# A four-layer network on one core: two sums of the scan moved to GpSimd, its linear terms reordered, the expert result read out in four pieces, and two fp32 matrix stages of the retrieval layer made of half-precision products

## The chip, the cores and the metric

The kernel is one program for one core of one Trainium2 chip. The engines are TensorE (PE in the profile, its weight loads PEld), VectorE (DVE), ScalarE (ACT), GpSimd (POOL) and SyncE (SP, which here only issues transfers). The metric is device time in microseconds from the first to the last instruction, as the median of a few runs.

## The reference, cut to what matters

The whole is a residual network of four layers over a token tensor of 8 x 256 x 512 (`XT` in the kernel, channels on partitions). The change touches layers 1 and 2.

```
x = x + L0_ffn(L0_cond(x, ...))                 # attention and a mixture of experts, untouched
x = x + L1_ffn(L1_cond(cond, x))                # GRU over 256 steps, then a base matrix plus one of 8 low-rank experts
x = x + L2_ffn(L2_cond(cond, cond, x))          # FitzHugh-Nagumo network over 256 steps, then retrieval
x = x + L3_ffn(L3_cond(x, ...))                 # untouched

# L2_cond: for each of 256 steps, classical Runge-Kutta with four evaluations of
#   dq = q - q**3/3 - p + drive + tanh(q) @ coupling.T + bias ;  dp = EPS*(q + ALPHA - BETA*p)
# q and p are clipped to +-20; the sequence of q goes on.
# L2_ffn (8 heads, 4096 = 64 x 64 experts):
h  = silu(q_seq @ W_up.T + b_up)                # 512 -> 2048, "wide layer"
h  = h @ W_down.T + b_down                      # 2048 -> 256
sim -> top 8 of 64 twice -> top 8 of 64 pairs -> indices, softmax(sc)
z   = silu((h . down_embed[indices]) * softmax)
out = sum of z * up_embed[indices]              # 64 picked rows of 512 per token
```

## The kernel before, in words

**The scan (function `scan`, lines 576 to 970).** The GRU of layer 1 and the network of layer 2 run in one loop of 256 steps. The GRU and layer 1's experts are 17 steps ahead (`LEAD`): 17 GRU steps run alone, then each of 256 common steps `t` does step `t` of the network and GRU step `s=t+17`. State is 32 numbers on each of 128 partitions (4 blocks of channels x 8 sequences). All matrices are products of fp16 halves: with `hi` and `lo` parts, 16 matmuls of 32 columns with the low weights ("low") and 16 with the high weights ("high").

One evaluation `k` (0 to 3) is a ring: ScalarE takes two tanh of the new `q` (`kx` in fp16 L748, `Tt` in fp32 L749) and the square (L753); TensorE multiplies `kx` by the low weights (L639); VectorE forms the low half of tanh (`low_part`, L889); TensorE multiplies both halves by the high weights (L642); meanwhile VectorE computes the cubic term (`cubic`, L892), adds the linear terms and writes the sum beside the products in PSUM (`total`, "k_ps" rows of L807); then VectorE adds the three parts (`end`, TENSOR_REDUCE, L900) and the next evaluation starts. In the gaps TensorE runs the 96 matmuls of the three GRU gates in batches of 24, 28, 28 and 16 behind evaluations 0 to 3, then a share of layer 1's experts. The linear terms (`K2`, `X`, `W`, `Q`, `B0`, `G0`) are sums of `q` and `p` of the step, prepared one by one on VectorE between the others. All this is in program order on each engine, so the order of the VectorE statements in the loop (lines 906 to 968) decides when `total` and `end` run. The GRU's new state (`state_half`, L845) opens the batch behind evaluation 0.

Layer 1's experts work on blocks of 8 steps (`TL=8`; i = s mod 8): router and low-rank matmuls at i = 0 and 1, base matrix at i = 0 to 4, on VectorE the choice of the expert at i = 2 and 3 (`experts`, L855 to L864, both parts ahead of `end` of evaluation 2), a transpose at i = 3, the expert matrix at i = 5 and 6, and at i = 7 ScalarE copies the result of 256 columns from PSUM (`expert_out`, L738, behind evaluation 1), whereupon GpSimd adds it into `XT` (`results`, L778).

GpSimd's queue in a step: `E0` (needs the new `p`), two operations for the next drive (`D`, `Ds`), and one copy of `q` into the sequence buffer `HQ` (L799).

**Retrieval (function `retrieve_experts`, lines 972 to 1326).** After the scan, three parts, all of whose TensorE work is in fp32. (1) 8 slices of 256 tokens: `up` (512 matmul records of 256 columns a half, L1048), `down` (L1061), `similar` (L1069), while VectorE picks the best keys. (2) 16 tiles of 128 tokens: dense products with `down_embed` (`dense`), picking by one-hot matmuls (`pick`). (3) 16 tiles: for tile i+1, `scatter` spreads the 64 weights of each token over 4096 rows (one-hot matmuls, L1107, four quarters a tile) and ScalarE copies the result to SBUF (`spread`, two operations a quarter, L1175); for tile i, `combine` multiplies that by the whole `up_embed` table (L1117, 32 chunks of rows x 4 blocks of channels). TensorE's order is scatter(i+1,q), combine(i,q) for q = 0 to 3. VectorE writes the one-hot tables (`pairs_hot`, L1288, four a tile) and, once all four scatters of tile i+1 are done, the weight table `AW` for the next tile (`weights_hot`, L1293 and L1294), on which the next scatter waits. The table `ue` (8 loads of 1 MB) arrives while the last picks run.

## Time and profile before

| | us |
|---|---|
| median of 3 runs | 4984.41 (4960.73 to 4988.18) |
| the profiled execution | 4976.67 |
| its span, first to last instruction | 4975.1 |
| TensorE busy | 4722.6 (95%) |
| VectorE busy | 2745.3 (55%) |
| ScalarE busy | 1688.9 (34%) |
| GpSimd busy | 435.9 (9%) |

TensorE is busy nearly everywhere, but matmuls are pipelined and a busy TensorE need not be the one that sets the time: in the scan the four engines pass the state round in a ring. The span has these stages: up to 1012 us layer 0, the gates' input products and the GRU's lead; 1012 to 2821 us the common scan (in its last 17 steps there are no gates); 2821 to 3227 us part (1) of the retrieval, to 3605 part (2), to 4231 part (3) with the part's start up to 3679; then layer 3.

### The profile page before, as it was taken

Reading aid. Unit: us, or ns where it says so; the run is one execution under the profiler, and the core shown is the slowest. Engines: PE = TensorE matmul, PEld = TensorE weight load, DVE = VectorE, ACT = ScalarE, POOL = GpSimd, SP = SyncE. Lnnn points to the kernel's source line nnn. Section 1 sums busy time; section 2 is a strip of 40 time slices with the busy share of each in tenths; the row PEclk is TensorE's granted clock in tenths of the full one; section 3 lists DMA queues with packets and bytes.
Section 4 is the critical chain, followed back from the end, with each engine's and each line's share of the span. In section 5 each row is a group of like instructions: output and inputs, shape, how many; then the busy total and the mean of one; then the engine's idle time right before and its main releaser. Section 6 shows DMA issues by size and latency. Waiting matters only on the chain. (4 is left out here: it accounts for less than half of the span.)

```text
span 4975.1 us, 200432 instructions
## 1 busy us (share of the span) xinstructions
PE 4722.6 (95%) x85104; PEld 3682.8 (74%) x85104; DVE 2745.3 (55%) x15135; ACT 1688.9 (34%) x7079; POOL 435.9 (9%) x1163
## 2 busy tenths in 40 slices
PE   8999989599999999999999799999999999999999
PEld 3435654489989999999998687789999999344444
DVE  4110011488888889888888545665543431344421
ACT  1101111145555555555555322233322221243320
POOL 1000010311111111111111100000000000000000
PEclk8899989799999999999998699999989999899999
DMA  3202430000000000000001000033310000100000
GB/s 102 98 25 87 169 123 22 15 5 5 5 5 5 5 5 5 5 5 5 5 5 55 13 10 1 36 90 92 98 58 3 3 3 2 47 9 8 10 7 34
DMA packets 52304, 159.81 MB, mean 32 GB/s; under 512 B 13873, under 2 KB 14001, under 8 KB 46272
## 3 DMA queue, kind: packets, MB, share of 16 engines
q1 hardware_dynamic: 45408, 130.70, 8.0%
q8 instruction: 662, 10.85, 0.9%
q0 software_dynamic: 3712, 12.29, 0.8%
q10 hardware_dynamic: 2304, 4.20, 0.2%
q14 instruction: 218, 1.79, 0.1%
HBM read 129.63 MB, written 17.17 MB: 30 GB/s over the span
## 5 line engine op out<-in xcount | busy, mean ns | idle before, releaser
L639 PE MATMUL k_ps<-k_hx,k_wlo 128*128 128x32 f16 x16384 | 585.2, 178 | 90.8 <-ACT k_hx L748 78.0
L639 PEld LDWEIGHTS k_ps<-k_hx,k_wlo 128*128 128x128 f16 x16384 | 490.2, 97 | 158.6 <-ACT k_hx L748 97.6
L642 PE MATMUL k_ps<-k_hl,k_whi 128*128 128x32 f16 x16384 | 578.0, 177 | 6.1 <-issue 3.9
L642 PEld LDWEIGHTS k_ps<-k_hl,k_whi 128*128 128x128 f16 x16384 | 496.0, 96 | 11.7 <-issue 8.6
L639 PE MATMUL g_ps<-g_HX,g_wlo 128*128 128x32 f16 x12240 | 426.0, 177 | 35.5 <-DVE g_HX L845 33.3
L642 PE MATMUL g_ps<-g_HL,g_whi 128*128 128x32 f16 x12240 | 425.3, 177 | 14.4 <-DVE g_HL L813 12.5
L639 PEld LDWEIGHTS g_ps<-g_HX,g_wlo 128*128 128x128 f16 x12240 | 361.3, 96 | 51.1 <-DVE g_HX L845 35.9
L642 PEld LDWEIGHTS g_ps<-g_HL,g_whi 128*128 128x128 f16 x12240 | 363.2, 96 | 17.1 <-DVE g_HL L813 12.7
L748 ACT ACTIVATE k_hx<-k_q 128x32 f16<-128x32 f32 x768 | 176.1, 229 | 529.3 <-DVE k_q L900 529.3
L1517 DVE TENSOR_REDUCE t_NM<-t_ps 128x1 f32<-128x512 f32 x256 | 165.0, 686 | 218.3 <-PE t_ps L1383 218.3
L1288 DVE TENSOR_TENSOR HQ<-p_ior,p_pm 128x2048 f32<-128x2048 f32 x61 | 139.4, 2290 | 218.5 <-PE p_sim L1107 218.5
L490 DVE TENSOR_TENSOR m_hT<-GRZ,m_ps 128x256 f32<-128x256 f32 (+1 forms) x72 | 36.6, 508 | 386.0 <-ACT GRZ L453 386.0
L1117 PE MATMUL p_dn<-wm,GRZ 128*128 128x128 f32 x2048 | 241.7, 280 | 2.0 <-ACT wm L1175 2.0
L1117 PEld LDWEIGHTS p_dn<-wm,GRZ 128*128 128x128 f32 x2048 | 235.6, 195 | 3.4 <-ACT wm L1175 2.2
L1117 PE MATMUL p_pq<-r_mem,GRZ 128*128 128x128 f32 x2048 | 236.3, 276 | 0.0
L751 ACT ACTIVATE k_hl<-k_hx 128x32 f16<-128x32 f16 x1024 | 234.1, 229 | 0.0
L1117 PEld LDWEIGHTS p_pq<-r_mem,GRZ 128*128 128x128 f32 x2048 | 230.9, 192 | 1.1
L900 DVE TENSOR_REDUCE k_q<-k_ps 128x32 f32<-128x96 f32 x768 | 197.2, 257 | 54.8 <-PE k_ps L642 34.2
L1048 PE MATMUL p_up<-HQ,GRZ 128*128 128x256 f32 x1024 | 225.2, 382 | 1.8 <-PEq L22 1.8
L753 ACT ACTIVATE k_sq<-k_q 128x32 f32<-128x32 f32 x1024 | 221.8, 217 | 2.0 <-DVE k_q L905 1.1
L1048 PEld LDWEIGHTS p_up<-HQ,GRZ 128*128 128x128 f32 x1024 | 196.4, 192 | 29.1 <-issue 1.9
L889 DVE CUSTOM_DVE_ANT_0 k_hl<-k_T,k_hx 128x32 f16<-128x32 f32 x1024 | 194.3, 190 | 28.4 <-ACT k_T L749 3.6
(359 smaller groups left out, 9252.9 us busy)
## 6 DMA issues: line engine op xcount, KB each, us to landing
GRZ<-expert_places SPq DMA_DIRECT2D x64, 512.0 KB, 5.0
wm<-in_w_dram SPq DMA_DIRECT2D x4, 2816.0 KB, 9.9
...
```

The source lines that it names most:

```text
L490: V.tensor_tensor(hT[0:M,m,0:n],sA[0:M,st,0:n],ps[st*2+1][0:M,0:n],ALU.mult).then_inc(s_h,1)
L639: T.matmul(P(j),lo[:,kc,(m0+j)*128:(m0+j+1)*128],bc(x[:,kc,:].unsqueeze(1),[128,4,NB]),start=(j==0 and kc==0),stop=False,skip_group_check= ...
L642: i=T.matmul(P(j),hi[:,kc,(m0+j)*128:(m0+j+1)*128],bc(x(kc).unsqueeze(1),[128,2,2,NB]),start=False,stop=kc==KC-1,skip_group_check=True)
L748: A.activation(kx[:],m4(src),ACT.Tanh,scale=uq[k]).then_inc(k_hi,1)
L751: A.activation(kl[:,:,0,:],kx[:],ACT.Copy,scale=S).then_inc(k_hS,1)
L753: A.activation(sq[:],q[:,k,:],ACT.Square,scale=uq[k]).then_inc(k_sq,1)
L889: V.tensor_tensor_reduce(kl[:,:,1,:],m4(Tt[:]),kx[:],S,0.0,ALU.subtract,ALU.max,lz[:,0:1]).then_inc(k_lo,1)
L900: V.tensor_reduce(qn[:] if k==3 else q[:,k+1,:],ksum(k),AX.X,ALU.add).then_inc(k_q,1)
L1048: x=T.matmul(psu[n%2][:,(m%2)*256:(m%2+1)*256],wup[:,dd,m*128:(m+1)*128],HQ[:,dd,s*256:(s+1)*256],start=dd==0,stop=dd==3)
L1117: x=T.matmul(pso[i%2][:,dd*128:(dd+1)*128],ue[:,cc,dd*128:(dd+1)*128],Ws[i%2][:,cc,:],start=cc==0 and dd==0,stop=cc==31,skip_group_check=True)
L1288: V.tensor_tensor(B0[q] if i==0 else Bp[:,q],bc(ior[:].unsqueeze(1),[128,16,128]),bc(PM[:,i,1,q*16:(q+1)*16].unsqueeze(2),[128,16,128]),AL ...
L1517: V.tensor_reduce(NM[:,qc,hh*64+32:hh*64+33],psX[hh][:,:],AX.X,ALU.max,negate=True).then_inc(s_mx,1)
```

## The change

Scan:

```diff
 # GpSimd
-    G.tensor_copy(HQ[:,:,:,t-1],m4(q[:,0,:])).then_inc(k_out,1)
+    state_out(t-1)
+ e.wait_ge(k_b,t*2+1)
+ G.tensor_tensor(K2[:],Q[:,0,:],B0[:,0,:],ALU.add).then_inc(k_kx,1)
+ e.wait_ge(k_b,t*2+2)
+ G.tensor_tensor(X[:,0,:],Q[:,0,:],B0[:,1,:],ALU.add).then_inc(k_kx,1)
  results(t+LEAD)
+def state_out(t):
+    if t>0: e.wait_ge(k_ol,t)
+    G.tensor_scalar(qs[:],q[:,0,:],uq[0]*SQ,None,ALU.mult).then_inc(k_out,1)
+    e.wait_ge(k_out,t+1)
+    G.tensor_copy(HP[:,:,:,t,0],m4(qs[:])).then_inc(k_oh,1)
+    e.wait_ge(k_oh,t+1)
+    G.tensor_tensor(HP[:,:,:,t,1],m4(qs[:]),HP[:,:,:,t,0],ALU.subtract).then_inc(k_ol,1)
 # VectorE, evaluation 0
-    pre(s-1,Z_); limit(t-1); arg(s-1,Z_); low_part(t,0); diff(s-1)
-    G0; Q0; upd(s-1); cubic(t,0); state_half(s-1); total(t,0)
+    pre(s-1,Z_); limit(t-1); low_part(t,0); arg(s-1,Z_); diff(s-1)
+    G0; Q0; cubic(t,0); upd(s-1); total(t,0); state_half(s-1)
     end(t,0)
 # evaluation 1
-    ...; low(s); K2; X0; cubic(t,1); Q2; total(t,1); W0; end(t,1)
+    ...; low(s); cubic(t,1); e.wait_ge(k_kx,t*2+1); Q2; total(t,1); end(t,1)
 # evaluation 2
-    X1; W1; low_part(t,2); pre(s,R_); arg(s,R_); cubic(t,2); X2; total(t,2); W2; experts(s,0); experts(s,1); end(t,2)
+    W0; e.wait_ge(k_kx,t*2+2); X1; low_part(t,2); W1; pre(s,R_); cubic(t,2); arg(s,R_); X2; total(t,2); experts(s,0); end(t,2)
 # evaluation 3
-    pn; X3; hid_n(s); low_part(t,3); reset(s); cubic(t,3); cand(s); p; total(t,3); end(t,3)
+    W2; X3; hid_n(s); low_part(t,3); reset(s); pn; cubic(t,3); cand(s); total(t,3); p; experts(s,1); end(t,3)
 # TensorE: the transpose of the experts
-    if i==3: base(7,11); e.wait_ge(l_ht,j+1); T.transpose(...)
-    if i==4: base(11,16)
+    if i==3: base(7,11)
+    if i==4: base(11,16); e.wait_ge(l_ht,j+1); T.transpose(...)
 # ScalarE: masked(s) at i==5 (was 4); expert_out(s,k) behind the square of every evaluation k, 64 columns each
-    A.activation(ex[:]...,pso[:,0:KC*TN],ACT.Copy,scale=US).then_inc(l_e,1)
+    A.activation(ex[:,dc]...,pso[:,dc*TN:(dc+1)*TN],ACT.Copy,scale=US).then_inc(l_e,1)
 # GpSimd: results(s) waits for the fourth piece, e.wait_ge(l_e,4*j+4)
```

`HP` is the buffer `HQ` seen as pairs of fp16 numbers, high and low, so neighbouring tokens of one half are 4 bytes apart.

Retrieval:

```diff
 # before part (1): W_up is split in place, chunk by chunk (4 chunks of 2048 elements a partition)
+for x in range(4):                       # ScalarE; waits for the VectorE step of chunk x-1
+    A.activation(wpair(x)[:,:,0,:],wup[:,:,x*512:(x+1)*512],ACT.Copy,scale=SW).then_inc(s_wh,1)
+for x in range(4):                       # VectorE
+    V.scalar_tensor_tensor(wpair(x)[:,:,1,:],wup[:,:,x*512:(x+1)*512],SW,wpair(x)[:,:,0,:],ALU.mult,ALU.subtract).then_inc(s_wl,1)
 # up
+if s==0 and m%4==0: e.wait_ge(s_wl,m//4+1)
-x=T.matmul(psu...,wup[:,dd,m*128:(m+1)*128],HQ[:,dd,s*256:(s+1)*256],start=dd==0,stop=dd==3)
+T.matmul(P,wh,qh,...); T.matmul(P,wh,ql,...); x=T.matmul(P,wl,qh,...)
 # combine
-if i==0 and cc%4==0: e.wait_ge(s_ue[cc//4],16)
+if i==0 and cc%4==0: e.wait_ge(s_ul,cc//4+1)
-x=T.matmul(pso...,ue[:,cc,dd*128:(dd+1)*128],Ws[i%2][:,cc,:],...)
+T.matmul(P,uh,Wp[i%2][:,0,cc,:],...); T.matmul(P,uh,Wp[i%2][:,1,cc,:],...); x=T.matmul(P,ul,Wp[i%2][:,0,cc,:],...)
 # spread: ScalarE writes the high half in fp16, VectorE the low half
-A.activation(Ws[i%2]...,psw[b][n%2]...,ACT.Copy).then_inc(s_wc,1)
+A.activation(Wp[i%2][:,0,...],psw[b][n%2]...,ACT.Copy,scale=CW).then_inc(s_Wh,1)
+def spread_low(i,q): for b in range(2): e.wait_ge(s_Wh,2*n+b+1); V.scalar_tensor_tensor(Wp[i%2][:,1,...],psw[b][n%2]...,CW,Wp[i%2][:,0,...],ALU.mult,ALU.subtract).then_inc(s_wc,1)
 # the table in 8 parts of 2048 elements, in place; table_high(x) waits for table_low(x-1)
+def table_high(x): ... A.activation(upair(x)[:,0]...,mem[:,x*2048:(x+1)*2048],ACT.Copy,scale=SW).then_inc(s_uh,1)
+def table_low(x): e.wait_ge(s_uh,x+1); V.scalar_tensor_tensor(upair(x)[:,1]...,mem[:,x*2048:(x+1)*2048],SW,upair(x)[:,0]...,ALU.mult,ALU.subtract).then_inc(s_ul,1)
 # VectorE order of part (3)
+if i==NTL-1: spread_low(0,q)            # in the last tile of part (2), behind product and pairs_hot of q
-for q in range(3): pairs_hot(4*i+8+q)
+for q in range(4):
+    if i==0: table_low(2*q); table_low(2*q+1)
+    spread_low(i+1,q)
+    if q<3: pairs_hot(4*i+8+q)
 weights_hot(i+2); pairs_hot(4*i+11); result(i)
```

On ScalarE `table_high(2q)` and `table_high(2q+1)` stand ahead of `spread(1,q)`. The result of a tile is scaled back in the operation that adds it to `XT`.

## Rows read from the trace of the kernel before

**Rows 1.** Windows, one for a stage: window, length; busy of PE, PEld, DVE, ACT, POOL; clock; DMA.

```profile
1012.30:2704.60 1692.30, 1629.20 (x55566) 1536.92 (x55567) 1512.65 (x11820) 889.84 (x5555) 267.89 (x982) 0.98 0.02 5
2821.40:3227.40 406.00, 400.54 (x1840) 326.34 (x1841) 206.53 (x1304) 102.78 (x200) 0.34 (x2) 0.99 0.05 18
3604.80:3678.80 74.00, 64.87 (x1476) 63.46 (x1473) 40.34 (x22) 15.71 (x18) 0.00 (x0) 0.79 0.27 108
3678.80:4231.00 552.20, 551.70 (x11009) 542.58 (x11008) 188.42 (x94) 111.12 (x112) 0.00 (x0) 1.00 0.01 3
```

**Rows 2.** Timeline, evaluations 0 and 1 of one step: start us, length us, engine, line, operation.

```profile
1504.05 0.55 PE L642 MATMUL k_ps<-k_hl,k_whi 128*128 128x32 f16 x16
...
1504.35 0.19 DVE L845 TENSOR_TENSOR g_HX<-g_m,g_n 128x32 f16<-128x32 f32 x1
...
1504.45 0.19 DVE L807 SCALAR_TENSOR_TENSOR k_ps<-k_g,k_Q 128x32 f32<-128x32 f32 x1
...
1504.59 0.77 PE L639 MATMUL g_ps<-g_HX,g_wlo 128*128 128x32 f16 x24
...
1504.75 0.26 DVE L900 TENSOR_REDUCE k_q<-k_ps 128x32 f32<-128x96 f32 x1
...
1505.77 0.55 PE L642 MATMUL k_ps<-k_hl,k_whi 128*128 128x32 f16 x16
...
1506.17 0.20 DVE L807 SCALAR_TENSOR_TENSOR k_ps<-k_g,k_Q 128x32 f32<-128x32 f32 x1
...
1506.47 0.26 DVE L900 TENSOR_REDUCE k_q<-k_ps 128x32 f32<-128x96 f32 x1
```

**Rows 3.** Timeline, evaluation 3 of the step before.

```profile
1502.37 0.55 PE L642 MATMUL k_ps<-k_hl,k_whi 128*128 128x32 f16 x16
...
1502.65 0.20 DVE L807 SCALAR_TENSOR_TENSOR k_ps<-k_g,k_X 128x32 f32<-128x32 f32 x1
...
1502.96 0.26 DVE L900 TENSOR_REDUCE k_qn<-k_ps 128x32 f32<-128x96 f32 x1
```

**Rows 4.** Timeline, the choice of the expert ahead of an evaluation's reduction.

```profile
1486.17 0.20 DVE L807 SCALAR_TENSOR_TENSOR k_ps<-k_g,k_Q 128x32 f32<-128x32 f32 x1
...
1486.83 0.24 DVE L900 TENSOR_REDUCE k_q<-k_ps 128x32 f32<-128x96 f32 x1
```

**Rows 5.** Timeline, GpSimd's addition of an expert result and VectorE beside it.

```profile
1739.72 0.88 POOL L778 TENSOR_TENSOR XT<-l_ex,XT 128x256 f32<-128x256 f32 x1 [2.02 <-ACT l_ex L738]
1739.77 0.87 DVE L807 SCALAR_TENSOR_TENSOR k_Q<-k_q,k_K 128x32 f32<-128x32 f32 x1
```

**Rows 6.** Timeline, GpSimd's copy of the state and VectorE beside it.

```profile
1503.75 0.24 POOL L799 COPY HQ<-k_q 128x32 f32<-128x32 f32 x1
...
1503.81 0.19 DVE L837 TENSOR_TENSOR g_d<-g_HF,g_n 128x32 f32<-128x32 f32 x1
```

**Rows 7.** Timeline, TensorE alone: the wide layer, and a quarter of `combine`.

```profile
2967.94 7.29 PE L1048 MATMUL p_up<-HQ,GRZ 128*128 128x256 f32 x33
...
3699.80 7.09 PE L1117 MATMUL p_pq<-r_mem,GRZ 128*128 128x128 f32 x62
```

**Rows 8.** Timeline, fp16 matmuls of 136 columns, back to back.

```profile
1524.40 0.22 PE L682 MATMUL l_psh<-wm,g_HL 128*64 128x136 f16 x1
...
1524.46 0.22 PE L683 MATMUL l_psh<-wm,g_HX 128*64 128x136 f16 x1
```

**Rows 9.** Groups by form on DVE and ACT: count, busy us, mean ns, idle before, releaser.

```profile
L568 DVE SCALAR_TENSOR_TENSOR g_wc<-g_wc,g_whi 128x2048 f32<-128x2048 f32 x3 | 6.9, 2292 | 0.1
...
L1274 DVE TENSOR_TENSOR GRZ<-p_sim,GRZ 128x512 f32<-128x512 f32 x64 | 44.2, 691 | 149.1 <-PE p_sim L1095 147.7
...
L1468 ACT ACTIVATE t_PT<-t_ps 128x512 f32<-128x512 f32 x256 | 139.1, 594 | 157.8 <-PE t_ps L1405 153.4
...
L1175 ACT ACTIVATE wm<-p_sim 128x512 f32<-128x512 f32 x32 | 35.6, 1112 | 0.0
```

**Rows 10.** Timeline on DVE, the end of the first weight table made in part (3).

```profile
3641.97 2.29 DVE L1294 TENSOR_TENSOR p_sel<-p_sel,p_pm 128x2048 f32<-128x2048 f32 x1
```

More of the change, by code:

```diff
@@ L952, in _ @@
                 total(t,2,Q[:,2,:],n_Q2)
+                experts(s,0)
+                end(t,2)
+                ch.after(n_X)
                 n_W=ch.did(stt(W[:,2,:],q[:,2,:],a*hh*(2-2*kap),W[:,1,:]))
-                experts(s,0); experts(s,1)
-                end(t,2)
-                ch.after(max(n_W,n_X))
-                n_p=ch.did(stt(pn[:],q[:,3,:],h*hh,W[:,2,:]))
                 n_X=ch.did(stt(X[:,3,:],q[:,3,:],2.0,X[:,2,:]))
@@ L962, in _ @@
                 reset(s)
+                ch.after(n_W)
+                n_p=ch.did(stt(pn[:],q[:,3,:],h*hh,W[:,2,:]))
                 cubic(t,3)
                 cand(s)
+                total(t,3,X[:,3,:],n_X)
                 ch.after(n_p)
                 V.tensor_scalar(p[:],pn[:],(20.0-SHIFT)/US,(-20.0-SHIFT)/US,ALU.min,ALU.max).then_inc(k_p,1)
-                total(t,3,X[:,3,:],n_X)
+                experts(s,1)
                 end(t,3)
@@ L1199, in _ @@
             for i in range(1,NTL):
-                for q in range(4): spread(i,q)
+                for q in range(4):
+                    if i==1: table_high(2*q); table_high(2*q+1)
+                    spread(i,q)
         @b_.vector
```

103 lines of the change are left out of this document (68 added, 35 removed).

## The prediction

> **What bounds the kernel now.** I read the windows by stage first, then the timeline of single steps of the scan, then the groups by form. The windows [rows 1] show two kinds of stage. In the retrieval's part (1) TensorE is busy 400.5 of 406.0 us and in part (3) 551.7 of 552.2 at full clock: the matrix products are the bound there. In the scan with gates (1692 us for 239 steps, 7.08 us each) TensorE is busy 1629 and VectorE 1513 us, so the timeline has to tell. What the reader is to see there is what the reduction that closes an evaluation came behind. In evaluation 3 the last high product ends at 1502.37+0.55=1502.92 and the reduction starts 0.04 us later, at 1502.96; `total` had ended at 1502.85, 0.11 before [rows 3]. That is TensorE's ring at its shortest. In evaluation 0 the products end at 1504.60 but the reduction starts at 1504.75, 0.11 behind the end of `total` (1504.45+0.19); in evaluation 1 products end 1506.32, `total` ends 1506.37, the reduction starts 1506.47 [rows 2]. So evaluations 0 and 1 are late by 0.11 us each, by the place of `total` in VectorE's queue, which starts an operation some 0.10 us behind the last. The choice of the expert adds more, twice in eight steps: `total` starts 1486.17, and without the two operations the reduction would start 0.30 behind it, at 1486.47, but it starts at 1486.83 [rows 4], 0.36 later; I take 0.24 for the other step (i=2), whose two operations are shorter. And once in eight steps GpSimd's addition of the expert result (0.88 us) holds a VectorE operation for its whole length, 0.87 where its like take 0.18 [rows 5].
>
> **The scan, evaluations 0 and 1.** Evaluation 0: `g_az` goes behind `low_part`, one place earlier for `low_part`, whose input tanh then ends it; `cubic` moves before `upd`. `total` needs the cubic term, which now starts one place (0.10) earlier, about 1504.17 by a pitch of 0.10 from its old 1504.23, less the wait on tanh: it ends 1504.35, `total` can start 0.035 later, 1504.39, and the reduction 0.30 behind that, 1504.69. Gain 0.06. But `state_half` (old start 1504.35) now stands behind `total`, so at 1504.50, 0.15 later, and it opens the batch of 24 gate products at 1504.59 [rows 2]. These take (0.77-0.18)/23=0.026 us each, 0.62 together, so TensorE is free at 1505.36 rather than 1505.21, while the next low products were due at 1505.32 and would now be at 1505.26. They start at 1505.36: the gain of evaluation 0 turns into 0.04 us lost. Evaluation 1: without `K2` and `X0` its `total` is two places earlier, 1505.97; the reduction is then TensorE's: from 1505.36 sixteen low products take 0.40, the sixteen high ones 0.55 with their drain, and 0.04 more [rows 2, 3]: 1506.35 against 1506.47. Evaluations 0 and 1 together gain 0.11 to 0.12 us a step. In steps whose evaluation 0 is late on TensorE because of experts' matmuls it is the same sum with the gain in evaluation 1 alone. Evaluation 2 gains 0.01, evaluation 3 nothing (`total` goes ahead of `p`, but `pn` and `cand` ahead of it: same place).
>
> **Experts.** `experts(s,0)` stays ahead of the reduction of evaluation 2, but one operation of 0.15 is covered; `experts(s,1)` now stands behind `p` in evaluation 3, where it costs about 0.04 (i=2) and 0.16 (i=3, a 0.34 us operation). Net over a block of eight steps: 0.24+0.36-0.04-0.16=0.40 us. The transpose moves from i=3 to i=4, behind 15 matmuls in place of 12: the next evaluation 0 is earlier once and later once, 0.02 lost. The four pieces: each is a short ScalarE operation behind the square, in a gap. But GpSimd's 0.88 us addition now waits for the fourth piece, in evaluation 3; `cand` (two inputs) and `total` then stand behind it, as [rows 5] shows for evaluation 1. The stall of about 0.66 us a block moves; it doesn't go.
>
> Sum: 8 x 0.12 + 8 x 0.01 + 0.40 - 0.02 = 1.42 us a block, 0.18 a step, x 239 = 42 us; at half clock TensorE binds sooner, so **40**. The last 17 steps have no gates and gain nothing.
>
> **GpSimd's new operations.** Per step it gets four more (three for one copy, two sums), each about 0.25 to 0.3 us (0.24 for 32 columns, 0.88 for 256 [rows 5, 6]); its queue stays under half full. `K2` is ready about 0.35 us behind `k_b`, before `Q2` wants it. What they do to VectorE is bounded by 0 (a copy of 0.24 starts at 1503.75, an operation with two inputs starts inside it and takes its usual 0.19 [rows 6]) and by their whole length [rows 5]. I take 0: the short copy is the nearest row. The Trainium skill ("SBUF — State Buffer", Who interferes with whom) says that a VectorE instruction with two SBUF inputs and a GpSimd instruction that reads SBUF exclude each other for the whole instruction. By that rule [rows 5] agree and [rows 6] do not; it would take back some 0.15 us a step. The rival below has the sum from rows.
>
> **Part (1).** 33 fp32 records of 256 columns take (7.29-0.38)/32=0.216 each, two a product, 0.432 [rows 7]. The fp16 matmuls start 0.06 apart at 136 columns [rows 8], (0.059 from six of them), 0.43 a thousand columns at full rate; so 0.109 at 256 columns, three of them 0.327. Per slice 64 x 0.105=6.7 us, x 8 = 54. Against it the splitting of W_up: per chunk one ScalarE operation of 2048 elements (1.7, if of the 0.594 for 512 some 0.2 is fixed, at most 2.4 [rows 9]) and one VectorE operation, 2.29 (2292 ns, the same operation on the same shape [rows 9]), alternating: 4.0 a chunk. TensorE starts 4 us late and, since ScalarE is in the chunks until about 14 us and two banks are all it has, it stops after four blocks until 16 us (with a table load): together 10 us, the cover being the four blocks. Net **-44**.
>
> **Part (3).** A quarter of `combine` is 64 records at (7.09-0.28)/61=0.112: 7.15 us [rows 7]; with the 2.0 us of a scatter 9.3, four of them 37.3, x 14 + 29 = 552, the window [rows 1]. New: 96 x 0.056=5.35 us. But the weight table comes late: behind the fourth scatter ScalarE writes two halves (ready after 1.15 and 2.0 us), VectorE two low halves of length d, and only then AW, 4.6 us (2 x 2.29). d is 0.69 (512 elements from PSUM) at least; if writing with a stride costs VectorE what it costs ScalarE (1112-594 [rows 9]), 1.2; I take 1.0, between. AW is ready at 7.75 us, TensorE wants it at 5.3: a new wait of 2.45 us per tile (before, 4.7 of AW lay under 7.2 of products). So tile: 4 x 7.35 + 2.45 = 31.85 instead of 37.3. 14 x 29.4 + 13 x 2.45 + 21.4 = 465 instead of 552; with some half-clock stretches after the waits (+7, a guess from the 0.79 clock of the part's start [rows 1]) 472: **-80**.
>
> Its start: AW for tile 1 was ready at 3644.26 [rows 10]; `spread_low(0,3)` now stands ahead of the last reductions, +6. Then per pair of table parts: 1.6+2.3 on ScalarE and VectorE by turns, half a quarter of products, scatter, spread, low, `pairs_hot`, next `table_low`: 16.3 us a round at full clock, up to 21 at half. 3652.6 + 3 x 16.3 + 9.6 = 3711 to 3725, taken 3718, where the second tile's scatter began at 3678.8: **+39**. Part (3) in all -41.
>
> **Sum.** 40+44+41=125 us. The profiled execution took 4976.67 (span 4975.1); 4976.7-125=4852. The median of the runs shown lies 8 us above it, so 4852 to 4860; I say **4855**.
>
> **Rivals.** (a) *GpSimd holds VectorE.* For: [rows 5]. Against: [rows 6]. If the short ones hold too, evaluation 0 has the scaling and the copy in front of `cubic` and `total`, 0.12+0.03 us by their overlap; evaluation 1 has the sums, inside TensorE's slack of 0.09. 0.15 x 239 = 36: 4891. (b) *The strided low halves are slow*, d=2.0: the wait grows to 4.45, 13 x 2 = 26, the start by 4: 4885. Speaks for it the ScalarE row; against, no VectorE row shows it. (c) *Slower than before: TensorE reads the pairs of fp16 numbers at half rate.* `up`'s moving operand is every second fp16 number; no row shows such a read. 3 x 0.216=0.65 per product against 0.432, +0.22 x 512 = 112 us where I count -54: 4855+166=5021. It decides from 0.19 us a product of 256 columns. Against: the same bytes are fetched as in fp32, where a pass takes 0.107. (d) *Better*: d=0.69, no half-clock stretches, rounds at full clock: -13-7-7: 4828. That the change doesn't do what it says: the GpSimd stall stays, as said, and is in the sum.
>
> **Chances.** Forecast 0.55, (a) 0.15, (b) 0.11, (c) 0.04, (d) 0.12, the rest (0.03) something between. The likeliest case alone: 4835 to 4875. For 8 in 10 the range reaches (d) and (a) with what lies beside: 4805 to 4905. What a measurement can tell from no change is about 0.5%, 25 us (the three runs of before spread 27). Faster by more: 0.92; within: 0.03; slower: 0.05, nearly all (c).
>
> **What would show it.** Step 6.90 us in the scan with gates; reduction 0.04 behind the products in evaluations 0 (with experts' work before it) and 1, and the low products of evaluation 1 waiting for TensorE, not for tanh; the 0.88 us hold now in evaluation 3; wide layer at 0.109 us a matmul; in part (3) TensorE waiting 2 to 3 us on `p_sel` once a tile. Wrong: if `end` of evaluation 0 or 1 still follows `total` by 0.10, if VectorE operations in the scan stretch beside GpSimd's, or if part (3) is bounded by VectorE throughout.

## The result, and the profile after

The changed kernel is slower, by under 1%: 5008.37 us (median of seven runs, 4999.8 to 5027.09) against 4972.69 (seven runs on the same chip, 4960.73 to 4988.18). The ratio is 1.0077, with an interval from 1.006 to 1.0093. The forecast was 4855, with a range to 4905.

The profiled executions (4975.1 and 5016.1 us of span) can be laid beside each other landmark by landmark. "Before" and "after" are lengths of stretches read from the two traces, in us:

| stretch | before | after | difference | forecast |
|---|---|---|---|---|
| start to the first half state of the gates (code unchanged) | 922.2 | 933.7 | +11.5 | 0 |
| lead to the common scan | 90.1 | 90.9 | +0.8 | 0 |
| scan, 256 steps | 1807.6 | 1791.2 | -16.4 | -40 |
| part (1), to the last write of hT | 400.6 | 365.9 | -34.7 | -44 |
| part (2), to the first `spread` | 386.4 | 387.8 | +1.4 | 0 |
| part (3), first `spread` to the first `result` | 72.7 | 131.1 | +58.4 | +39 |
| part (3), the other 15 tiles | 551.6 | 575.9 | +24.3 | -80 |
| layer 3 (code unchanged) | 743.8 | 739.6 | -4.2 | 0 |

The two unchanged stretches are no effect. In the thirteen kernels below, none of which touches layer 0, the first one took 913.3 to 935.6 us and the last 739.3 to 750.1, so differences under some 10 us there belong to the single execution. The stretches of the retrieval repeat to within 2 us, those of the scan to within 6.

Four windows of the kernel after, for [rows 1]; the columns are those there.

```profile
1024.60:2704.00 1679.40, 1600.65 (x55641) 1534.20 (x55642) 1488.95 (x11365) 915.70 (x5659) 579.04 (x1943) 0.97 0.02 5
2822.60:3188.00 365.40, 355.20 (x2350) 278.64 (x2351) 212.94 (x1303) 108.21 (x203) 0.00 (x0) 0.98 0.05 17
3566.20:3702.30 136.10, 67.38 (x1779) 65.53 (x1776) 98.06 (x49) 53.29 (x27) 0.00 (x0) 0.63 0.16 62
3702.30:4275.80 573.50, 484.70 (x12794) 473.90 (x12792) 456.73 (x204) 264.72 (x112) 0.00 (x0) 0.89 0.01 3
```

The last window is the one to read. TensorE was busy in 551.7 of 552.2 us [rows 1]; now it is idle for 89 of 573, at a clock of 0.89, while VectorE went from 188 to 457 us busy and ScalarE from 111 to 265. Who it waits for is in the waits of that window (engine and line that waited, engine and line that ended it, us, times, longest), and what made it late in the groups by form:

```profile
PE p_up L1130 <- DVE p_sel L1332: 84.6, 13, 6.6
```

```profile
L1202 ACT ACTIVATE r_mem<-p_sim 128x512 f16<-128x512 f32 x28 | 77.9, 2781 | 0.0
...
L1343 DVE SCALAR_TENSOR_TENSOR r_mem<-p_sim,r_mem 128x512 f16<-128x512 f32 x28 | 76.2, 2720 | 0.0
L1343 DVE SCALAR_TENSOR_TENSOR r_mem<-p_up,r_mem 128x512 f16<-128x512 f32 x28 | 73.2, 2613 | 51.8 <-ACT r_mem L1202 51.8
...
L1202 ACT ACTIVATE r_mem<-p_up 128x512 f16<-128x512 f32 x28 | 69.0, 2463 | 147.9 <-PE p_sim L1130 147.9
```

Thirteen tiles wait 6.5 us each for the weight table AW (84.6 us in all). That is not the whole price. Behind each of these waits the granted clock stands at the lower of its two levels (1.2 GHz, 0.50 in the rows) for 5 to 8.5 us. One wait and what follows it, as windows with the columns of [rows 1]:

```profile
3731.00:3737.60 6.60, 0.03 (x3) 0.01 (x2) 6.57 (x4) 0.00 (x0) 0.00 (x0) 0.82 0.00 0
3737.60:3745.40 7.80, 7.80 (x169) 7.74 (x169) 4.37 (x3) 4.11 (x2) 0.00 (x0) 0.50 0.01 2
3745.40:3771.00 25.60, 25.60 (x730) 25.08 (x728) 22.55 (x11) 14.86 (x7) 0.00 (x0) 1.00 0.02 4
```

AW is late because `spread` takes 2.46 and 2.78 us for 512 numbers, where it took 1.11 in fp32 [rows 9], and `spread_low` takes 2.61 and 2.72, where 0.69 to 1.2 had been allowed. The chain of one tile, VectorE first, then the two ScalarE operations ahead of it (start, length):

```profile
4007.35 2.61 DVE L1343 SCALAR_TENSOR_TENSOR r_mem<-p_up,r_mem 128x512 f16<-128x512 f32 x1 [0.60 <-ACT r_mem L1202]
4009.63 2.71 DVE L1343 SCALAR_TENSOR_TENSOR r_mem<-p_sim,r_mem 128x512 f16<-128x512 f32 x1
4011.93 2.52 DVE L1331 TENSOR_TENSOR p_sel<-p_ior,p_pm 128x2048 f32<-128x2048 f32 x1
...
4004.85 2.46 ACT L1202 ACTIVATE r_mem<-p_up 128x512 f16<-128x512 f32 x1 [3.00 <-PE p_sim L1130]
4006.80 2.79 ACT L1202 ACTIVATE r_mem<-p_sim 128x512 f16<-128x512 f32 x1
```

From the end of the scatter at 4004.8 to the start of AW there are 7.1 us, where the forecast had 3.15. The forecast's other term for a tile was right: a matmul of 128 columns starts 0.056 us behind the last.

In the scan, `L812` and `L814` are the two sums on GpSimd, `L904` is `low_part`, the row `k_Q<-k_G,k_Q` is `Q1`. Evaluation 1 of one step (start, length), VectorE and then GpSimd:

```profile
1531.60 0.29 DVE L904 CUSTOM_DVE_ANT_0 k_hl<-k_T,k_hx 128x32 f16<-128x32 f32 x1
...
1531.83 0.28 DVE L822 SCALAR_TENSOR_TENSOR k_Q<-k_G,k_Q 128x32 f32<-128x32 f32 x1
1532.03 0.18 DVE L828 SCALAR_TENSOR_TENSOR g_HL<-g_HF,g_HL 128x32 f16<-128x32 f32 x1
...
1532.34 0.20 DVE L822 SCALAR_TENSOR_TENSOR k_ps<-k_g,k_Q 128x32 f32<-128x32 f32 x1
1532.64 0.26 DVE L915 TENSOR_REDUCE k_q<-k_ps 128x32 f32<-128x96 f32 x1
...
1531.60 0.25 POOL L812 TENSOR_TENSOR k_K<-k_Q,k_B 128x32 f32<-128x32 f32 x1 [0.28 <-DVE k_B L822]
1531.81 0.25 POOL L814 TENSOR_TENSOR k_X<-k_Q,k_B 128x32 f32<-128x32 f32 x1
```

`low_part` has 0.29 where its like have 0.19, and `Q1` 0.28 where its like have 0.19. `total` (k_ps) starts 1.12 us into the evaluation although two operations were taken from in front of it, and the reduction still follows `total` by 0.10, as in [rows 2]. Evaluation 3 of the step with the expert result, GpSimd and VectorE, is [rows 5] in its new place:

```profile
1521.00 0.91 POOL L782 TENSOR_TENSOR XT<-l_ex,XT 128x256 f32<-128x256 f32 x1 [3.16 <-ACT l_ex L740]
```

```profile
1521.08 0.88 DVE L822 SCALAR_TENSOR_TENSOR g_w<-g_t,HQ 128x32 f32<-128x32 f32 x1
```

### The profile page after: what moved, and what is told of

Same layout as the page of the kernel before. It is cut to its first block and busy times, and to the rows that moved or that the text cites. A ratio compares the mean times of both kernels' runs of the same rounds, so it can differ in the third digit from the quotient of the medians.

```text
span 5016.1 us, 206672 instructions
## 1 busy us (share of the span) xinstructions
PE 4589.0 (91%) x87664; PEld 3565.8 (71%) x87664; DVE 3051.3 (61%) x14763; ACT 1911.1 (38%) x7187; POOL 767.0 (15%) x2187
## 5 line engine op out<-in xcount | busy, mean ns | idle before, releaser
L643 PE MATMUL g_ps<-g_HL,g_whi 128*128 128x32 f16 x12240 | 426.9, 177 | 15.9 <-DVE g_HL L828 12.5
L904 DVE CUSTOM_DVE_ANT_0 k_hl<-k_T,k_hx 128x32 f16<-128x32 f32 x1024 | 212.4, 207 | 37.0 <-ACT k_T L752 10.2
L1130 PE MATMUL p_up<-p_sel,HQ 64*64 64x32 f32 x3904 | 149.4, 237 | 91.4 <-DVE p_sel L1332 91.2
L1130 PEld LDWEIGHTS p_up<-p_sel,HQ 64*64 64x64 f32 x3904 | 142.2, 156 | 98.7 <-DVE p_sel L1332 93.6
L806 POOL TENSOR_TENSOR k_E<-k_Ds,k_p 128x32 f32<-128x32 f32 x256 | 64.4, 251 | 881.9 <-DVE k_p L979 881.7
L1523 ACT ACTIVATE t_PT<-t_ps 128x512 f32<-128x512 f32 x256 | 138.9, 595 | 155.1 <-PE t_ps L1460 150.5
L907 DVE SCALAR_TENSOR_TENSOR k_g<-k_sq,k_q 128x32 f32<-128x32 f32 x1024 | 194.1, 190 | 0.0
L1142 PE MATMUL p_dn<-wm,GRZ 128*128 128x128 f16 x896 | 158.4, 224 | 32.8 <-DVE GRZ L1346 32.6
```

The lines of the kernel that those rows point to most:

```text
L643: i=T.matmul(P(j),hi[:,kc,(m0+j)*128:(m0+j+1)*128],bc(x(kc).unsqueeze(1),[128,2,2,NB]),start=False,stop=kc==KC-1,skip_group_check=True)
L904: V.tensor_tensor_reduce(kl[:,:,1,:],m4(Tt[:]),kx[:],S,0.0,ALU.subtract,ALU.max,lz[:,0:1]).then_inc(k_lo,1)
L907: at['g']=ch.did(V.scalar_tensor_tensor(g[:],sq[:],-3.0,q[:,k,:],ALU.add,ALU.mult))
L1130: x=T.matmul(psw[b][n%2][h*64:(h+1)*64,j*32:(j+1)*32],hot[b*64:(b+1)*64,j,h*64:(h+1)*64],AW[b*64:(b+1)*64,q*16+j,:],start=True,stop=True)
L1142: T.matmul(P,uh,Wp[i%2][:,0,cc,:],start=cc==0 and dd==0,stop=False,skip_group_check=True)
L1523: A.activation(PT[:,kc,hh,:],psE[hh][:,:],ACT.Exp).then_inc(s_e,1)
```

## Experiments: part (3)

The experiments are numbered in the order in which they ran, as the expectations count them.

**One fp16 number every 256 bytes (experiments 1 and 2).** Two kernels keep every instruction of the changed kernel and change only addresses. The first lays the weights out so that both engines write 512 fp16 numbers in one run, and TensorE reads every 64 bytes:

```
-Wp=[x.bitcast(F16).rearrange('p (s c t) -> p s c t',s=2,t=128) ...
+Wp=[x.bitcast(F16).rearrange('p (s t c) -> p s c t',s=2,t=128) ...
```

> The changed kernel with one line edited: the fp16 pair of weights that `combine` reads is laid out (t c) in place of (c t), so that ScalarE's spread and VectorE's spread_low write 512 fp16 numbers one behind the other, and TensorE reads its moving operand every 64 bytes. Theory A (fp16 numbers written every 256 bytes are what costs): spread falls from 2.45-2.8 us to about 0.6-0.7, spread_low from 2.6-2.75 to 0.7-0.8, the AW table is ready some 6.5 us behind the fourth scatter, TensorE waits about 1 us a tile, a tile takes 30 to 32 us in place of 40, the tiles of part (3) 440 to 470 us in place of 573, the start 110 to 125 in place of 136: whole kernel 4880 to 4900. Rival B (the price is in the fp16 output or in the PSUM read, whatever the stride): both stay at 2.4-2.8 us, the time at 5008. Rival C (TensorE reads a moving operand with a 64-byte stride at half rate or less): combine's matmuls of 128 columns take 0.11 in place of 0.056 us each, a quarter 10 us, tiles 48 us: 5100 or more.

5924.43 us, 1.1889 of before (1.1866 to 1.1912), 1000 us above what theory A said for the whole. About the writes theory A is right: `spread` fell to 0.59 and 0.60 us, `spread_low` to 0.68 and 0.69. But TensorE pays for it: a combine matmul starts 0.217 us behind the last, four times 0.056 (rival C, which had it at twice). The timeline of TensorE, and a window of the middle of part (3):

```profile
4000.25 0.39 PE L1143 MATMUL p_pq<-r_mem,GRZ 128*128 128x128 f16 x1
4000.47 0.39 PE L1144 MATMUL p_pq<-r_mem,GRZ 128*128 128x128 f16 x1
4000.68 0.39 PE L1142 MATMUL p_pq<-r_mem,GRZ 128*128 128x128 f16 x1
```

```profile
3900.00:4400.00 500.00, 500.00 (x4535) 310.83 (x4532) 103.66 (x80) 22.81 (x42) 0.00 (x0) 0.50 0.00 1
```

The granted clock is 0.50, the lower of the two levels (1.2 GHz), in all of 1440 us, although TensorE shows as busy throughout. A factor of two goes with the clock: in the changed kernel, with the same clock, combine matmuls with contiguous reads start 0.107 us apart. The other factor of two is the reads. Why the clock stayed low was not tested.

```profile
3980.46 0.31 PE L1144 MATMUL p_dn<-wm 128*128 128x128 f16 x1
3980.57 0.31 PE L1142 MATMUL p_dn<-wm 128*128 128x128 f16 x1
```

The second keeps the layout and turns the loop inside the instruction: PSUM is read every 128 bytes, and 16 fp16 numbers are written in a row.

```
-Wp[i%2][:,0,:,y].rearrange('p c j -> p j c'), psw[b][n%2].rearrange('p (j c) -> p j c',c=32)
+Wp[i%2][:,0,:,y],                             psw[b][n%2].rearrange('p (j c) -> p c j',c=32)
```

> The changed kernel with the same layout (c t) of the fp16 pair, but spread and spread_low go through it c by c: 16 numbers in a row are written (32 bytes), and PSUM is read every 128 bytes. Theory A (isolated fp16 writes cost): both fall to between 0.6 and 1.2 us, a tile to about 32, part (3)'s tiles to 450-480 us, the kernel to about 4900. Rival B (output type): they stay at 2.4-2.8. Rival D (any stride on either side costs as much, reading PSUM too): they stay at 2 us or more.

4887.62 us in one run (4984.0 for the kernel before, measured beside it). Groups by form of this kernel:

```profile
L1343 DVE SCALAR_TENSOR_TENSOR r_mem<-p_up,r_mem 128x512 f16<-128x512 f32 x32 | 22.1, 692 | 111.1 <-ACT r_mem L1202 111.0
...
L1202 ACT ACTIVATE wm<-p_up 128x512 f16<-128x512 f32 x32 | 19.1, 597 | 217.7 <-PE p_sim L1130 217.7
```

These are the lengths of contiguous operations [rows 9], so PSUM read with a stride costs nothing here, and B and D fall. From the second `result` to the last, fourteen tiles, it took 426.6 us, 30.5 each, in place of 536.2 (before: 514.2). The last tile has no scatter and is shorter; between two results in the middle lie 31.5 us here, 40 in the changed kernel and 37.4 in the one before. The first `result` came 859.9 us behind the scan in place of 884.8. By the landmarks of the table this edit of addresses is worth 142 us: 25 in the start (105.9 against 131.1) and 117 in the other 15 tiles (459.2 against 575.9). The whole kernel shows 121 of them in this one run; the scan happened to take 6 us more.

```profile
3676.10:4136.10 460.00, 443.47 (x12866) 432.41 (x12860) 255.02 (x206) 60.79 (x112) 0.00 (x0) 1.00 0.01 4
```

Beside the window of the changed kernel above (484.70 busy of 573.50 at 0.89) this splits the gain in the tiles: some 71 us less waiting for AW (13.1 in place of 84.6), and 41 us less busy time for the same products, at a clock of 1.00. A wait of 1 us a tile did not bring the clock down; one of 6.5 did.

**Pairs (8).** Is it the distance or the size of the write? ScalarE alone writes two fp16 numbers (4 bytes) every 256 bytes:

```
-Wp[i%2][:,0,:,y],                                        ...'p (j c) -> p c j'
+Wp[i%2][:,0,:,y].rearrange('p c (j y) -> p j c y',y=2),  ...'p (j y c) -> p j c y'
```

> The kernel with runs of 16, where ScalarE alone writes the high halves as pairs of fp16 numbers (4 bytes every 256) in place of runs of 16 (32 bytes); VectorE's low halves stay in runs of 16. Theory A1 (what costs is a write of less than 4 bytes by itself): about 0.6 to 1.1 us for 512 numbers, as fp32 numbers with a stride had 1.08 to 1.11. Rival A2 (what costs is the number of separate places written, whatever their size): half of 2.45-2.78, some 1.3 us. Rival A3 (the stride of 256 bytes itself costs by the element): 2.4 or more.

```profile
L1202 ACT ACTIVATE wm<-p_up 128x512 f16<-128x512 f32 x32 | 19.7, 615 | 217.4 <-PE p_sim L1130 217.4
```

0.615 and 0.602: as good as runs; the kernel took 4858.85 us in one run. So it is the lone 2-byte write, at some (2460-600)/512 = 3.6 ns a number above a run, not the stride (A1). VectorE was not run with pairs. A lone fp32 number every 512 bytes cost ScalarE 1.1 us for 512 [rows 9], more than 512 numbers in pairs of fp16. The Trainium skill ("Advanced Engine Details and Errata", SBUF Cachelines) says that accesses need at least two hits on a 16-byte line to absorb the latency; fp16 pairs against single fp16 numbers agree with it (0.615 against 2.46 us). For fp32 there are only single numbers (1.1) and runs (0.594) to compare; pairs of fp32 were not run.

**The products themselves (3).** Part (3) alone as before:

```
-3 fp16 matmuls from Wp, upair; spread_low, table_high, table_low; scaled result
+1 fp32 matmul from Ws, ue; result by addition
```

> The changed kernel with part (3) alone as before (the fp32 table and weights, one product in place of three, no spread_low, no table_high and table_low). Theory: part (3) is where 83 us of the loss sit: its start 74 and its tiles 552 us again (changed kernel: 136 and 573 in the profiled execution), the rest stays: about 4925 us, 0.990 of the kernel before. Rival (the scan, part (1) and layer 0 as read from one profiled execution are off by run-to-run differences of 10 to 20 us): anything from 4905 to 4950.

4936.45 us, 0.9912 (0.989 to 0.9935). First `spread` to first `result` is 73.1, the other tiles 551: as in the kernel before. Part (3) as changed costs 83 us, and the rest of the change gains about 44 against before.

**What was left of the waits (7).** With runs of 16, TensorE waited 13.1 us in thirteen tiles for AW, and the start still took 33 us more than before. The next kernel, on that of experiment 2, makes AW in two halves of 1.22 us operations, of which the first lets the scatter start, and splits table parts 0 and 1 during the last tile of part (2), the others between the first scatters:

```
-e.wait_ge(s_aw,i+1)                    # scatter
+e.wait_ge(s_aw,2*i+1+q//2)
-for q in range(4): table_high(2*q); table_high(2*q+1); spread(1,q)
+table_high(0), (1) beside spread(0,1), (0,2); then 2, 3, spread(1,0), 4, spread(1,1), 5, 6, ...
```

> The kernel with runs of 16, with AW written in two halves (its first half lets the next scatter start) and the table split earlier: parts 0 and 1 during the last tile of part (2), the rest between the first scatters of part (3). Theory: what is left of the loss in part (3) is the wait for AW (1.07 us a tile: 30.47 against 4 x 7.35) and the chain of the eight table parts at 4.2 us each in front of the products. Tiles 29.4 to 29.7 us each (14 of them 412 to 416 in place of 427), the end of the first tile's result 20 to 35 us earlier than 860 us behind the scan: 35 to 45 us less than 4887, about 4845. Rival: VectorE is the bound of the tile (2.29 x 6 + 8 x 0.69 + ... = 21 us, no) or TensorE's half-clock stretches at the start take back most of it: 10 to 15 us less only.

4833.25 us, 0.9699 (0.9681 to 0.9718). The same fourteen tiles 408.7, 29.2 each (29.9 in the middle, where the forecast's sum without a wait is 4 x 7.35 = 29.4); the first `result` at 831.5, 28 earlier. TensorE is busy 421.2 of 422.2 us:

```profile
3646.60:4068.80 422.20, 421.21 (x12524) 412.12 (x12521) 258.96 (x233) 60.78 (x112) 0.00 (x0) 0.99 0.02 4
```

## Experiments: the scan and part (1)

**The two sums, back on VectorE (4)**, on the changed kernel, in their old place:

```
-G.tensor_tensor(K2[:],...).then_inc(k_kx,1); G.tensor_tensor(X[:,0,:],...)
+n_K=ch.did(V.tensor_tensor(K2[:],...)); n_X0=ch.did(V.tensor_tensor(X[:,0,:],...))
```

> The changed kernel with the two sums K2 and X0 on VectorE again, in their old place ahead of cubic in evaluation 1. Theory H (VectorE's operations wait for the whole length of the two sums that GpSimd runs in evaluation 1, 0.26 us each, so moving them there gained nothing): the period of evaluation 1 stays at 1.71-1.73 us, the whole at 5005-5015. Rival I (nothing is held; total of evaluation 1 is late for another reason, such as low_part itself being slow): two more operations of 0.10 us each ahead of total, the period becomes 1.90, +0.19 x 239 = +45 us, 5053.

5022.54 us, 1.0083 (1.005 to 1.0115). The period of an evaluation is counted from the end of one reduction to the end of the next. That of evaluation 1 (median of steps without experts' work) is 1.725 us against 1.716: moving them gained 0.01, where two operations of 0.10 had been taken away. Rival I wanted 1.90. And **without them (5)**, in the kernel with runs of 16 (the additions K2 and X0 of the integration are left out, VectorE reads constants):

> The kernel with runs of 16 (the second experiment), without the two sums K2 and X0: GpSimd does not issue them, VectorE reads constants in their place (that part of the integration is left out), every other instruction stays. Theory H (these two GpSimd additions hold VectorE for their length in evaluation 1): the period of evaluation 1 falls from 1.716 to between 1.61 and 1.65 us, low_part is followed after 0.12 and not after 0.22 us, total ends 0.10 earlier; scan about 239 x 0.08 = 20 us shorter. Rival I (nothing is held): the period stays at 1.71.

```profile
1531.75 0.19 DVE L902 CUSTOM_DVE_ANT_0 k_hl<-k_T,k_hx 128x32 f16<-128x32 f32 x1
...
1531.87 0.19 DVE L818 SCALAR_TENSOR_TENSOR k_Q<-k_G,k_Q 128x32 f32<-128x32 f32 x1
...
1532.30 0.20 DVE L818 SCALAR_TENSOR_TENSOR k_ps<-k_g,k_Q 128x32 f32<-128x32 f32 x1
1532.69 0.26 DVE L913 TENSOR_REDUCE k_q<-k_ps 128x32 f32<-128x96 f32 x1 [0.19 <-PE k_ps L643]
```

Both operations have their 0.19 again, `total` starts at 0.925 in place of 1.12, and the reduction waits for TensorE: period 1.61 in undisturbed steps and 1.65 to 1.68 in others. Theory H holds for the evaluation. The whole took 4886.15 us in one run, against 4887.62. The mean of evaluation 1 fell by 0.056 (1.740 to 1.684), but those of 2 and 3 rose by 0.011 and 0.014, so the scan became only 7 us shorter where 20 had been expected.

The traces say where the rest went. Add up, over 238 steps, the medians of each evaluation at its place in the block of eight: 1658.0 us in the kernel before, 1631.8 in the changed one, 1633.1 with runs of 16, 1617.8 without the sums. So the usual step gained 15 us from leaving them out. What real steps took above these medians grew at the same time, from 44 to 52 us; it was 29 in the kernel before and 39 in the changed one. Part of it are pauses of TensorE in the middle of a row of matmuls, for which the profile shows no wait:

```profile
1393.54 0.32 PE L640 MATMUL k_ps<-k_hx,k_wlo 128*128 128x32 f16 x6
1394.48 0.40 PE L640 MATMUL k_ps<-k_hx,k_wlo 128*128 128x32 f16 x10 [0.63 <-issue]
```

Pauses of this kind over 0.1 us number 57 in these steps of the kernel before (14 us), 79 in the changed one (21 us), 96 with runs of 16 (27 us) and 110 without the sums (34 us). What makes them, and why there are more, no run shows.

**The state in one operation (9)**: the kernel of experiment 7, part (1) and its feeding as before:

```
-three fp16 matmuls; qs, HP[...,0], HP[...,1] on GpSimd; halves of W_up
+one fp32 matmul; G.tensor_copy(HQ[:,:,:,t],m4(q[:,0,:]))
```

> The seventh experiment's kernel (AW in halves, tables early) with part (1) and what feeds it as before: fp32 products for `up`, no splitting of W_up, GpSimd copies the state once a step in place of three operations. Theory: part (1) is worth what the windows say, the last write of hT comes 400.6 us behind the scan again in place of 365-366 (35 us more); the scan stays at 1790-1802 us because the three GpSimd operations of evaluation 0 fall beside VectorE operations that are not last. Rival K (these three hold VectorE too, like the two sums): the scan gets shorter by up to 0.15 a step, to about 1765.

4865.83 us in one run. The last hT comes at 399.9 against 365.1, so part (1) is worth 35 us, as read. The scan took 1789.8 us, which other executions of the new order reach too. The surprise is in evaluation 1: it takes 1.63 to 1.65 us although both sums are there. VectorE, then GpSimd:

```profile
1518.57 0.19 DVE L899 CUSTOM_DVE_ANT_0 k_hl<-k_T,k_hx 128x32 f16<-128x32 f32 x1
...
1518.69 0.23 DVE L817 SCALAR_TENSOR_TENSOR k_Q<-k_G,k_Q 128x32 f32<-128x32 f32 x1
...
1518.57 0.31 POOL L807 TENSOR_TENSOR k_K<-k_Q,k_B 128x32 f32<-128x32 f32 x1 [1.39 <-DVE k_B L817]
1518.84 0.30 POOL L809 TENSOR_TENSOR k_X<-k_Q,k_B 128x32 f32<-128x32 f32 x1
```

Without the three operations ahead of it, K2 starts 0.381 us into the evaluation, with `low_part`, and not at 0.373; now GpSimd's sum is the one that stretches (0.31) and VectorE loses 0.11 in all, not 0.20. Part (1) and scan are tied by 8 ns. Why K2 starts these 8 ns later is not shown, but that they decide is: the changed kernel has both cases in one trace. In 155 of its steps `low_part` starts 6 to 11 ns behind K2 and takes 0.29, K2 0.25; in 61 it starts from 4 ns ahead of K2 to 5 behind and takes 0.19, K2 0.30 to 0.31.

**The scan's old order (12)**: the kernel of experiment 7, scan as before but for the state, which is written as a pair:

> The seventh experiment's kernel with the scan as before, but for the state, which GpSimd writes as a pair of fp16 numbers in three operations (part (1) needs it). Theory: the new order of the scan is worth about 10 us: 1806 to 1810 us for the scan in place of 1797 (mean of eight executions with the new order). Rival K (the three GpSimd operations cost in evaluation 0, and the new order made up for it): 1820 or more.

1810.0 us for the scan, 4859.17 in all. Six executions of the new order (the changed kernel and experiments 1, 2, 3, 7 and 8) lie between 1790.2 and 1802.1, mean 1797.0. So the new order is worth about 13 us against this one and 10 against the kernel before (1807.6). In the old order the three operations stretch evaluation 0 of quiet steps from 1.795 to 1.828 us. GpSimd and VectorE there:

```profile
1507.15 0.29 POOL L792 TENSOR_SCALAR k_qs<-k_q 128x32 f32<-128x32 f32 x1
```

```profile
1507.18 0.22 DVE L815 SCALAR_TENSOR_TENSOR k_G<-k_p,k_q 128x32 f32<-128x32 f32 x1
1507.33 0.18 DVE L815 SCALAR_TENSOR_TENSOR k_Q<-k_q,k_E 128x32 f32<-128x32 f32 x1
```

The scaling has started 0.03 us ahead, and the VectorE operation beside it takes 0.22 where its like take 0.18; the next starts 0.15 behind it and not 0.10.

**K2 later (13)**, on the kernel of experiment 11: whether it matters which engine starts first.

```
+e.wait_ge(k_lo,t*4+2)      # before GpSimd's K2
```

> The eleventh experiment's kernel, where GpSimd's first sum (K2) waits for the end of low_part of evaluation 1 as well, so that it starts at about 0.51 us of the evaluation in place of 0.373, 8 ns ahead of low_part. Theory S (a GpSimd addition that has started first keeps a two-input VectorE operation waiting, one that starts behind it or beside it costs half): low_part is followed after 0.12 us again in place of 0.22, total of evaluation 1 starts at 0.93 to 1.05 us in place of 1.12, the period 1.62 to 1.66; scan 6 to 13 us shorter than 1790. Rival O (every overlap costs the same, wherever it falls): the two sums hold the next operations (Q1, low, cubic) by the same 0.2 us in all; total at 1.12, period 1.71. Rival W: K2 comes too late for Q2 (end at 0.78 and 0.1 for the semaphore), total later than 1.12.

4826.76 us, 0.9684 (0.9658 to 0.971), scan 1795.9. `low_part` and `Q1` are free of holds (next operation after 0.12 and 0.10), and K2 and X0, which now start behind a VectorE operation, hold it for 0.04 at most. But K2 started only at 0.727 us, 0.15 behind the end it waited for (0.382+0.19), so `Q2` waited and `total` came at 1.19, the period at 1.768: rival W. Theory S is supported by the rows, and useless in this place: the kernel is no faster than that of experiment 11 (4824.19).

**The expert result in four pieces on GpSimd (6)**, on the kernel of experiment 2:

```
-G.tensor_tensor(x,ex[:],x,ALU.add).then_inc(l_x,1)
+for dc in range(KC): e.wait_ge(l_e,4*j+dc+1); G.tensor_tensor(XT[:,dc,...],ex[:,dc],...)
```

> The kernel with runs of 16, and GpSimd adds the expert result in four pieces of 64 columns, one behind each of ScalarE's four copies, in place of one of 256 behind the fourth. Theory H: one hold of 0.88 us in evaluation 3 of every eighth step (period 2.267 against 1.610) becomes four of about 0.25, two of them in evaluation 1 to 2, one in 2, one in 3, each costing 0 to 0.15: per eight steps 0.66 becomes 0.1 to 0.4, over 32 blocks 8 to 18 us less than the kernel with runs of 16. Rival: a hold costs its full length wherever it falls (4 x 0.25 = 1.0 us a block), which would be 11 us more.

4871.12 us, 0.9775 (0.9749 to 0.9802). The scan stayed (1798.2 against 1797.6). In the steps concerned evaluation 3 fell from 2.266 to 1.756, evaluation 1 rose from 1.717 to 2.125 and 2 by 0.07: of 0.66 us of hold, 0.62 were there again. Theory H had 0.1 to 0.4 and the rival 1.0; what was measured lies between: cut into pieces, the hold costs VectorE as much as whole.

**The same addition on VectorE (10)**, on the kernel of experiment 7:

```
-G.tensor_tensor(x,ex[:],x,ALU.add).then_inc(l_x,1)
+V.tensor_tensor(x,ex[:],x,ALU.add).then_inc(l_x,1)   # evaluation 3, behind total
```

> The seventh experiment's kernel where VectorE and not GpSimd adds the expert result, 256 columns once in eight steps, in evaluation 3 behind total. Theory H (what costs is that VectorE can't work for the whole 0.88 us of the GpSimd addition): VectorE's own addition takes about 0.35 us; the period of evaluation 3 in that step falls from 2.267 to about 1.95, 32 x 0.3 = 10 us less, about 4823. Rival: that step's evaluation is late for ScalarE's four pieces, not for the hold; the period stays above 2.2.

4821.15 us, 0.969 (0.9663 to 0.9718), not to be told from experiment 7. Evaluation 3 of that step takes 2.050 in place of 2.267, 32 x 0.217 = 7 us less, and not 0.3 less, because VectorE's addition takes 0.656 us, not 0.35. Its columns lie apart in XT; that this is what makes it slow was not tested.

```profile
L863 DVE TENSOR_TENSOR XT<-l_ex,XT 128x256 f32<-128x256 f32 x32 | 21.0, 656 | 0.0
```

**All together (11)**: that kernel, with W_up split in eight halves:

```
-for x in range(4): high of 2048 numbers; wait; low of 2048 numbers
+for n in range(8): high of 1024; low of 1024, behind each other on two engines
```

> The tenth experiment's kernel, and W_up split in eight halves of 1024 numbers in place of four chunks of 2048, so that ScalarE and VectorE work beside each other: TensorE starts 2.5 us behind the scan's end plus barrier, not 4.5, and ScalarE's first SiLU comes 4 to 5 us earlier. hT's last write 360 us behind the scan in place of 365, the whole about 4818, 0.967 of the kernel before. Rival: the start is bound by VectorE's low halves in total (8 x 1.2 = 9.6, as 4 x 2.3), then at most 2 us.

4824.19 us, 0.9688 (0.9661 to 0.9716, five runs). hT's last write comes at 359.4 in place of 366.0, TensorE starts 4.9 us behind the scan in place of 6.8. The total doesn't show these 6 us against its own spread. Of the kernels run, those of experiments 7, 10, 11 and 13 (4821 to 4833) are 3% faster than the one before and can't be ranked.

## Why the prediction was wrong

The profiled executions lie 166 us apart from the forecast (+41 where -125 had been said). Part (3) is 124 of them (104 in the tiles, 19 in the start), the scan 24, part (1) 9, and 9 lie in stretches where no change was forecast.

**Part (3), the tiles: forecast -80, measured +24.** The step that failed is the length d of a low half, "0.69 at least, 1.2 if writing with a stride costs VectorE what it costs ScalarE, I take 1.0", and beside it the high half on ScalarE, left at its fp32 lengths. Both ends of the bound came from fp32 rows. No row of the trace before showed a lone fp16 number written, and I did not see that as an unknown with its own upper bound. Measured: d = 2.61 and 2.72, ScalarE 2.46 and 2.78. The wait for AW became 6.5 us a tile in place of 2.45, and this made a second term too small, the 7 us that had been guessed for half-clock stretches: TensorE's busy time in the tiles is 41 us longer than in experiment 2, with the clock at 0.50 behind each wait. Rival (b) had the mechanism, with d = 2.0 and ScalarE unchanged, and so 4885; "slower" had a chance of 0.05 and was put down to rival (c), which did not occur. With the writes in runs a tile takes 31.5, near the 31.85 of the forecast, by two misses that cancel: the wait was 1.0 us (13.1 in thirteen tiles) in place of 2.45, because d came out at 0.69 and ScalarE at 0.6, and the tile without it 30.5 in place of 29.4. `combine` took 0.056 a matmul, as forecast.

**Part (3), the start: forecast +39, measured +58** by the landmarks of the table, and +33 with writes in runs. The rounds were about right; the slow writes stood in each.

**Part (1): forecast -44, measured -34.7.** The fp16 matmul of 256 columns starts 0.1133 behind the last, not 0.109, 4% more: 512 x 3 x 0.0043 = 7 us. Whether reading every second fp16 number costs this or the 0.109, worked out from 136 columns, was too low is not shown: twice the 0.056 of 128 contiguous columns is 0.112. The timeline of the changed kernel:

```profile
3010.01 0.27 PE L1069 MATMUL p_up<-HQ,GRZ 128*128 128x256 f16 x1
3010.12 0.28 PE L1070 MATMUL p_up<-HQ,GRZ 128*128 128x256 f16 x1
3010.24 0.27 PE L1071 MATMUL p_up<-HQ,GRZ 128*128 128x256 f16 x1
```

The gain on the matmuls is 512 x (0.432-0.340) = 47 us, so the start cost 12.5, where I had 10. Rival (c) asked for half rate at this stride; it is wrong there, and right at a stride of 64 bytes, where nothing in this change reads (experiment 1).

**The scan: forecast -40, measured -16 in one execution, some -10 over six.** The means of the four evaluations went from 1858, 1819, 1748, 1659 to 1855, 1729, 1658, 1776 ns. The 0.66 us hold moved from evaluation 1 to 3 (0.08 a step), as forecast. Taken out, the means of evaluations 0 and 1 together gained 0.01 where 0.11 to 0.12 had been forecast. The step that failed is "they hold nothing, I take 0, the short copy is the nearest row". In steps whose evaluation 0 is late on TensorE the gain should have been in evaluation 1 alone; there it went from 1.722 to 1.716 with the sums and to 1.610 without them, 0.11 as forecast. In quiet steps evaluation 0 did gain the 0.06 of the forecast (1.795 to 1.736). By medians the scan without the sums gained 1658.0-1617.8 = 40 us, the forecast's own number; with them 26. Of what the scan missed, some 15 us are the two sums, and the rest is that real steps exceed their medians by more than before (experiment 5), for which the forecast had no term and no run has a cause. The nearest row was a copy, with one input; the sums have two, and a GpSimd addition with two inputs stood in [rows 5] with its full length. Rival (a) was right in kind; its sum put the loss into evaluation 0 (0.15) and saw evaluation 1 inside TensorE's slack, and it was the other way round: 0.03 in evaluation 0 (experiment 12), and in evaluation 1 0.20 of hold, which made its period up to 0.11 longer. The choice of the expert gained what had been forecast in evaluation 2 (1.872 and 1.992 us to 1.630) and gave back 0.12 in 3. The moved transpose was priced at 0.02 lost a block: evaluation 0 of the next step costs 0.157 more (1.797 to 1.954), and 0.092 less the step before, 0.065 lost.

The Trainium skill ("SBUF — State Buffer", Who interferes with whom) has a VectorE operation with two SBUF inputs and a GpSimd operation that reads SBUF exclude each other, and whichever starts first keeps the other waiting. The sums agree, in both directions (experiment 9). GpSimd's scaling of the state in evaluation 0, with one input from SBUF, agrees too, though it looks free at first. In the kernel after it starts with a VectorE operation, and that one has its usual 0.18, the next one 0.10 behind it. GpSimd, then VectorE:

```profile
1530.17 0.33 POOL L795 TENSOR_SCALAR k_qs<-k_q 128x32 f32<-128x32 f32 x1
```

```profile
1530.17 0.18 DVE L822 SCALAR_TENSOR_TENSOR k_Q<-k_q,k_E 128x32 f32<-128x32 f32 x1
1530.27 0.20 DVE L907 SCALAR_TENSOR_TENSOR k_g<-k_sq,k_q 128x32 f32<-128x32 f32 x1
```

But here GpSimd is the one that waits: 0.33 for the scaling (median 0.335 of 141 such steps), where it takes 0.29 when it has started first, and then VectorE's operation has 0.22 (experiment 12, 175 steps). So [rows 6] did not show that a copy holds nothing; its VectorE operation started 0.06 behind the copy, when most of the hold was over. Where GpSimd's operation of 32 columns had started first, it cost VectorE up to 0.06 with one input and 0.10 with two. Where VectorE's had, that one lost nothing, though the one behind it could (0.23 in place of 0.19 in experiment 9).

With runs, part (3) gives 33 in the start and takes 92 from the tiles (459.2 against 551.6): with 10 of the scan and 33 of parts (1) and (2) that is -102, 4973-102 = 4871. The three kernels of that kind measured 4887.62 and 4858.85 (one run each) and 4871.12. That lies in the range of the forecast, and 16 above its value, in part by luck: runs cost less than the d = 1.0 of the forecast (0.69), which covers some of what the scan and the parts without a change lost.
